# A two-layer recurrence with the loops of three engines written out

## The reference

```
# layer 0, from h = cond, c = 0
a = x_t @ Wx + b + h @ Wh            # 128 -> 4 * 128: i, f, o, g
c = sigmoid(f) * c + sigmoid(i) * tanh(g)
h = sigmoid(o) * tanh(c)
x1_t = x_t + h
# layer 1, from u = cond
m = concat(x1_t, u) @ weight + bias   # 256 -> 2 * 128: gate, candidate
g = sigmoid(m_gate + 1)
u = g * u + (1 - g) * tanh(m_cand)
out_t = x1_t + u
```

## Time and profile before

| what | value |
|---|---|
| median of 3 runs | 230.73 us (230.63 to 232.51) |
| the profiled execution | 230.85 us, span 229.3 us |
| granted TensorE clock, mean over the span | 0.994 |
| TensorE: matmul busy, weight load busy | 223.5 us, 207.8 us |
| VectorE, ScalarE, GpSimd busy | 201.3 us, 120.4 us, 4.0 us |
| transfers | 6.22 MB, mean 27 GB/s |

### The profile page before, as it was taken

One profiled execution on the slowest core, in us unless ns is written; L12 is line 12 of the kernel. 1 busy time (PEld: TensorE's weight loads), 2 busy tenths in 40 slices (PEclk: granted clock), 3 DMA queues, 4 the chain that ended last, 5 costly groups with the idle time before them and its releaser, 6 DMA issues.

```text
span 229.3 us, 12844 instructions
## 1 busy us (share of the span) xinstructions
PE 223.5 (97%) x4850; PEld 207.8 (91%) x4850; DVE 201.3 (88%) x1557; ACT 120.4 (52%) x774; POOL 4.0 (2%) x12
## 2 busy tenths in 40 slices
PE   6999999999999999999999999999999999999993
PEld 5899999999999999999999999999999999999882
DVE  6789989899899898898988998989989989899894
ACT  4445555555555555555555555555555555555551
POOL 1500000000000000000000000000000000000000
PEclk9999999999999999999999999999999999999997
DMA  5001001001010001000010000100001000100000
GB/s 191 19 16 27 18 24 49 14 27 30 21 37 23 22 13 46 23 11 23 23 34 23 23 11 23 46 11 23 23 21 36 23 23 11 27 14 14 16 14 13
DMA packets 11971, 6.22 MB, mean 27 GB/s; under 512 B 1447, under 2 KB 11693, under 8 KB 11949
## 3 DMA queue, kind: packets, MB, share of 16 engines
q1 hardware_dynamic: 11792, 5.66, 8.7%
q10 hardware_dynamic: 156, 0.27, 0.3%
HBM read 3.82 MB, written 2.10 MB: 26 GB/s over the span
## 4 chain that ended last, share of the span: by engine, by line
PE 73%; DVE 20%; ACT 3%; DMA 1%; issue 1%; SPq 1%
PE a L289 14%; PE gate_f L263 11%; PE a L247 7%; PE a L281 6%; PE gate_o L231 4%; PE gate_i L231 4%; PE gate_g L231 3%; DVE cell_bank L565 3%; PE gate_f L231 3%; PE gate_g L269 3%; PE gate_o L269 3%; PE gate_i L269 3%; ACT act_bank L480 3%; PE gate_i L273 2%; PE a L283 2%; DVE hT L572 2%
## 5 line engine op out<-in xcount | busy, mean ns | idle before, releaser
L263 PE MATMUL gate_f<-hT,wh_raw 128*128 128x32 f32 x254 | 48.9, 275 | 0.2
L263 PEld LDWEIGHTS gate_f<-hT,wh_raw 128*128 128x128 f32 x254 | 37.8, 188 | 11.5 <-DVE hT L572 7.8
L465 ACT ACTIVATE forget<-gate_f 128x32 f32<-128x32 f32 x127 | 25.1, 197 | 37.2 <-PE gate_f L263 37.1
L485 ACT ACTIVATE acts<-a 128x64 f32<-128x64 f32 x128 | 28.6, 223 | 28.3 <-PE a L289 28.3
L572 DVE TENSOR_TENSOR hT<-out_gate,act_bank 128x32 f32<-128x32 f32 x128 | 24.1, 188 | 21.6 <-ACT act_bank L480 21.6
L480 ACT ACTIVATE act_bank<-cell_bank 128x32 f32<-128x32 f32 x128 | 23.3, 182 | 35.8 <-DVE cell_bank L565 35.8
L565 DVE TENSOR_TENSOR_SCAN cell_bank<-scan_mul,scan_add 128x64 f32<-128x64 f32 x128 | 38.6, 302 | 0.3 <-ACT scan_add L465 0.3
L281 PE MATMUL a<-h_high,w1x_scaled 128*128 128x32 f16 x256 | 35.4, 176 | 0.1
L281 PE MATMUL a<-h_high,w1x_third 128*128 128x32 f16 x256 | 35.4, 176 | 0.0
L281 PE MATMUL a<-h_high,w1x_rest 128*128 128x32 f16 x256 | 35.3, 176 | 0.0
L283 PE MATMUL a<-h_low,w1x_fp 128*128 128x32 f16 x256 | 35.3, 176 | 0.0
(11 more groups left out here) (102 smaller groups left out, 864.1 us busy)
## 6 DMA issues: line engine op xcount, KB each, us to landing
xT<-in_x_dram SPq DMA_DIRECT2D x46, 64.0 KB, 1.9
out_dram<-outT SPq DMA_DIRECT2D x32, 64.0 KB, 1.6
wx_s<-in_L_cond_Wx_dram SPq DMA_DIRECT2D x1, 256.0 KB, 2.8
wh_raw<-in_L_cond_Wh_dram ACTq DMA_DIRECT2D x1, 256.0 KB, 3.1
w_raw<-in_L_cond_weight_dram SPq DMA_DIRECT2D x1, 256.0 KB, 3.5
bias_rows<-in_biases_dram ACTq DMA_DIRECT2D x1, 3.0 KB
condT<-in_cond_dram SPq DMA_DIRECT2D x1, 16.0 KB, 3.1
```

Of the source, the lines that this page charges most:

```text
L263: nc.tensor.matmul(gate_step(GATE_F, j), wh_raw[:, GATE_F * P:(GATE_F + 1) * P], hT[:, (j - 1) % RING, :], start=False, stop=True, skip_gr ...
L465: return nc.scalar.activation(out, gate_step(q, j), func)
L485: nc.scalar.activation(acts1[:, 0:3:2, i, :], a1_step(j).rearrange("p (g n) -> p g n", g=2), ACT.Tanh).then_inc(acts1_ready, 1)
```

## The change

The Python function `schedule` no longer makes a loop on the engine. It calls `body` eight times, for s0 = 0, 16, ..., 112, with s0 a Python number, so all 128 steps are written out and every wait has a constant. VectorE's loop is changed in the same way. The instructions of each step, their order, their operands and their waits stay the same. SyncE's program and GpSimd's stay as they were.

```diff
-        def schedule(eng, body):
-            body(0, True, False)
-            with eng.Fori(BODY, T - BODY, BODY) as s0:
-                body(s0, False, False)
-            body(T - BODY, False, True)
+        def schedule(body):
+            for s0 in range(0, T, BODY):
+                body(s0, s0 == 0, s0 == T - BODY)
...
-            schedule(pe, body)
+            schedule(body)
...
-            schedule(act, body)
+            schedule(body)
...
-            body(0, True)
-            with dve.Fori(BODY, T - BODY, BODY) as s0:
-                body(s0, False)
-            body(T - BODY, False)
+            for s0 in range(0, T, BODY):
+                body(s0, s0 == 0)
```

## The result

The changed kernel takes 0.9953 of the time of the kernel before, with an interval of 0.9934 to 0.9971: a gain of some half per cent, small but clear. The forecast was 229.6 us after 230.73, also half a per cent. The medians of 20 executions each are 230.46 us (229.57 to 233.37) and 232.11 us (230.63 to 234.81). Medians are a poor measure here, because the executions of both kernels fall into levels some 1.4 us apart, and a median depends on how many fall into which. Before, 6 lie at 230.63 to 230.92 and 13 at 231.69 to 232.51, with one at 234.81. After, 10 lie at 229.57 to 230.10 and 9 at 230.82 to 231.50, with one at 233.37. Level against level it is 229.77 after 230.78, and 231.17 after 232.22: 1.0 us less in both.

The account below looks back on a forecast made before the run. The prediction took a 1.69 us ring through TensorE, ScalarE and VectorE as the bound; late steps of 1.02 + 0.08 + 0.07, taken as 1.2 us, off 230.85 or 230.73 gave 229.6 us, range 229.0 to 231.3.

Parts of the forecast that it names:

- The ring and the plain step: Each step's cycle through TensorE, ScalarE and VectorE, hT to next hT: 1.69 us, looped or written out; register work free there.
- The sum: Late steps in the looped stretch: 1.02 + 0.08 + 0.07 is 1.17 us, taken as 1.2, giving 229.6 us.
- What a measurement can tell: Whole kernel: about 1% distinguishable from no change, 228.4 to 233.0 us; within 1% got 0.90, faster by more 0.03.
- Back edges, 1.02 us: At the loop's five jumps back on each of three engines: late steps of 1.02 us in all would go.
- L613 at the entry, 0.08: Second step of the loop's first turn: VectorE's ALU_OP for the x wait makes it 0.08 us late; this goes.
- The single late step at 24, 0.07: First turn only, at 47.45 us: u_low late by 0.07 us, put down to new program arriving; taken as gone.
- Added program, 0: Instruction queues of the written-out program: up to 37 packets on q8 and 24 on q14, costing 0 on the path.
- rival A: Each new program piece on VectorE or ScalarE costs a 0.07 us late step; time 230.6 us; loop register work may matter; chance 0.08.
- Rival E: Each of five back edges fetches program at 1.3 us; gain 6.5 us, time 224.2 us; chance 0.01.
- the rule behind it: Trainium skill, "Instruction fetch mechanics": a taken branch to a place outside the two pages held forces a fetch.

Follow-up runs that it names:

- The kernel with no branch taken: Against the kernel before, the loop of six turns became six loops of one turn on TensorE, VectorE and ScalarE; steps 16 to 111 took 161.74 us, before 161.71.
- the three kernels with long loops: Loops of 32 steps to a turn: on TensorE, VectorE and ScalarE 243.44 us; TensorE alone, others written out, 239.84; VectorE and ScalarE, TensorE written out, 240.54.

## Why the prediction was right or wrong

*The ring and the plain step: right.* 1.69 us a step, written out or looped, and the register work of a plain step is free. The changed kernel shows it in all 128 steps.

*The sum: right.* The rows of before gave 1.16 to 1.25 us of late steps; 1.19 went. In the time of the whole kernel it was 1.0 us in each level and 1.06 in the profiled executions; 1.2 was forecast. Some 0.15 is missing: in the profile of after the first hT starts at 7.72 us against 7.42, and in the executions of the changed kernel's repeat and of the one with SyncE written out at 7.57 and 7.49. Whether writing out delays the start a little or this is scatter stays open. The forecast of 229.6 us lies in the lower level; the median of 230.46 stands between two levels, which three executions of before (230.63 to 232.51) had already hinted at and the prediction did not read. That its starting value, 230.73, lay in the lower level was luck: the median of twenty is 232.11.

*What a measurement can tell: wrong, and this is the step that failed.* The prediction said that "about 1% is what a measurement of this kernel can tell from no change", and so gave 0.90 to "within 1%" and 0.03 to faster by more, although its own sum was 0.5% faster. It gave no reason for the 1%; the only rows were three executions that lay 0.8% apart. The runs showed that 20 executions of each kernel tell some 0.2%: the interval is 0.9934 to 0.9971, and it leaves out 1. So does the interval of every further measurement with the three engines written out (they end at 0.9957 to 0.9979). Where the time goes and how much of it stood (the points below); what failed was taking a real gain of 0.5% for none.

*Back edges, 1.02 us: right in size, the cause only in part.* The prediction called it the price of five jumps back. The kernel with no branch taken kept 0.73 of 1.05 us (with one MOVE more at each edge than the kernel before); a large part is arithmetic and MOVEs on the sequencers of TensorE and VectorE, at places where they have no lead.

*L613 at the entry, 0.08: the size right, the cause double.* TensorE has 0.06 to 0.07 of its own there.

*The single late step at 24, 0.07: right,* it went, but for 0.02 at step 25. That new program arrives there is borne out: with VectorE's body fetched again in every turn it came back in every turn. Only the reading that u_low came late is wrong. These two rows stand ahead of it:

```profile
47.78 0.18 DVE L579 SCALAR_TENSOR_TENSOR h_low<-hT,h_high 128x32 f16<-128x32 f32 x1
48.01 0.19 DVE L586 SCALAR_TENSOR_TENSOR pair<-acts 128x32 f32<-128x32 f32 x1
```

VectorE's next product starts 0.23 us behind h_low; one step on it is 0.11 (49.54 to 49.65). The pause lies there, and a packet of q14 begins at 47.9.

*Added program, 0: right.* 38 packets on q8 (37 forecast) and 18 on q14 (24 forecast; these are of 8 KB, and not 16), with no late step but the 0.02 at step 25. The condition that the prediction named under rival A seems to decide it: with register work left in the program, new program went with late steps of 0.17 and 0.23 us on ScalarE and of 0.06 to 0.09 on VectorE. That the register work is what makes the difference is not tested by itself.

*Rival E and the rule behind it: rightly given nearly no chance for this kernel, but for too weak a reason.* I read 0.2 us per edge as evidence against the rule, and it was only evidence that this body is short enough. Twice the body costs 4 to 5 us per edge, and the branch alone 3.3 to 3.8, where rival E had put a fetch at 1.3.

## What to carry to other kernels

A kernel that has both a loop and written-out parts answers the question of unrolling by itself: compare the distances of one instruction in both, add up the late ones, and that sum is what can be won, as long as the added program costs nothing, which only a run can tell. A loop's cost sits on the sequencers at its edge, so a register instruction is best put where its engine is idle anyway and not between two products that another engine waits for. Don't lengthen a loop's body to save back edges without counting its instructions: here 16 steps to a turn cost 0.2 us an edge, 32 steps over 4 us, and no loop at all was best of the three.

## What the runs showed of the hardware

- TensorE's COMPARE_BRANCH took 0.215 us in the median when taken, 0.074 in one-turn loops and 0.083 at the end of the long one when not, and 3.3 to 3.8 us when the target had to be fetched. ScalarE's took 0.03 to 0.05 us throughout. VectorE's took 0.06 even in the long loop, and the fetch showed as 2.7 to 3.0 us of idle time behind it.
- A straight program of 38 packets of 16 KB, one about every 5.7 us, was fetched with no late step over 0.02 us, while the engines ran 97% and 88% busy.
- A standstill of TensorE of 2.5 to 3.5 us at a back edge went with 6.8 us at 1.2 GHz, at all six edges of the three kernels with long loops.
- The time at which the full clock came in the start (some 5, 10 or 16 us) goes with levels of the time; of the kernel before these lie at 230.78, 232.22 and 234.81 us.
